# Scores' left factor z of batches 3 to 15 by seven block products instead of eight, a two-slot ring for silu's output, the attention output told by halves, and new orders on every engine

## The reference, cut to what matters

```python
# x: (16, 1024, 256) fp32; all dims 256 except HIDDEN = 768
x = x + layernorm(attn(layernorm(x)))        # qkv = x W^T + b; softmax(Q K^T / 16) V, one head of 256
x = x + layernorm(ffn(layernorm(x)))         # h = silu(x Wg^T) * (x Wu^T); h Wd^T, weights are int32 / 127
```

## Time and profile before

| | |
|---|---|
| median of 3 runs | 1324.28 us (1322.99 to 1324.62) |
| the profiled execution's own time | 1322.73 us |
| its span (first to last instruction) | 1320.9 us |
| PE busy | 1308.1 us of the span |
| ACT, POOL, DVE busy | 1019.5, 997.6, 953.1 us |
| instructions | 23123, of them 7204 matmuls |

### The profile page before, as it was taken

How to read it: one execution, slowest core, us unless ns; L and a number is a source line. 1 busy time by engine, 2 the same in 40 slices (tenths; PEclk the granted TensorE clock), 3 DMA queues, 4 the chain that set the end, 5 groups by cost and what they waited for, 6 DMA issues and landing times.

```text
span 1320.9 us, 23123 instructions
## 1 busy us (share of the span) xinstructions
PE 1308.1 (99%) x7204; PEld 705.6 (53%) x7204; DVE 953.1 (72%) x2670; ACT 1019.5 (77%) x1610; POOL 997.6 (76%) x1081
## 2 busy tenths in 40 slices
PE   8999999999999999999999999999999999999998
PEld 5455455555555555455554555545555555555655
DVE  7877686776867768687686867767687686766566
ACT  6768787788878788787887877878777887867655
POOL 4887687786868868687786877878778686875645
PEclk9999999999999999999999999999999999999999
DMA  6887657676656865578666776666767666666422
GB/s 203 158 172 143 147 93 145 130 153 116 120 124 134 167 119 112 122 138 161 125 115 124 130 148 128 142 124 111 144 128 158 116 119 121 136 132 130 92 64 65
DMA packets 492110, 171.96 MB, mean 130 GB/s; under 512 B 473041, under 2 KB 475473, under 8 KB 491986
## 3 DMA queue, kind: packets, MB, share of 16 engines
q1 hardware_dynamic: 491184, 169.67, 65.1%
q10 hardware_dynamic: 802, 0.79, 0.2%
HBM read 36.70 MB, written 16.78 MB: 40 GB/s over the span
## 4 chain that ended last, share of the span: by engine, by line
PE 90%; POOL 3%; issue 2%; ACT 2%; DMA 2%; SPq 1%; DVE 1%; POOLq 0%; ACTq 0%; DVEq 0%
PE S L1073 71%; PE S L1232 17%; POOL Pl L449 1%; DMA yTl<-yl 1%; SPq L309 1%; DMA PTh<-Ph 1%; POOL qTl L426 0%; POOL yl L476 0%; PE S L1102 0%; PE S L1155 0%; ACT xh L558 0%; SPq L278 0%; ACT P L614 0%; SPq L321 0%; POOL xl L401 0%
## 5 line engine op out<-in xcount | busy, mean ns | idle before, releaser
L449 POOL TENSOR_TENSOR Pl<-P,Ph 128x1024 f16<-128x1024 f32 x128 | 271.4, 2131 | 52.4 <-issue 37.8
L1073 PE MATMUL S<-PTh,xh 128*128 128x512 f16 x512 | 194.1, 379 | 0.0
L1073 PE MATMUL S<-PTl,xh 128*128 128x512 f16 x512 | 194.0, 379 | 0.0
L1073 PE MATMUL S<-PTh,xl 128*128 128x512 f16 x512 | 194.0, 379 | 0.0
L651 ACT ACTIVATE hf<-S,sc 128x512 f32<-128x512 f32 x192 | 129.3, 684 | 64.8 <-PE S L1073 52.8
L614 ACT ACTIVATE P<-P,nmx,sc 128x1024 f32<-128x1024 f32 x112 | 138.2, 1234 | 43.4 <-DVE nmx L901 43.2
L1073 PE MATMUL S<-Wh,hTh 128*128 128x256 f16 x768 | 170.2, 273 | 0.4 <-DVE X L986 0.4
L1073 PE MATMUL S<-Wh,hTl 128*128 128x256 f16 x768 | 170.2, 273 | 0.0
L364 POOL TENSOR_TENSOR rs<-rs,mhalf 128x4 f32<-128x4 f32 (+2 forms) x160 | 146.0, 912 | 13.3
L485 POOL TENSOR_TENSOR hTl<-hf,hTh 128x512 f16<-128x512 f32 x128 | 146.8, 1157 | 8.6 <-ACT hTh L658 5.6
L895 DVE CUSTOM_DVE_ANT_0 P<-S,P 128x512 f32<-128x512 f32 x112 | 76.9, 689 | 96.7 <-ACT P L581 46.6
(11 more groups left out here) (206 smaller groups left out, 3295.6 us busy)
## 6 DMA issues: line engine op xcount, KB each, us to landing
xs<-in_L_attn_t SPq DMA_DIRECT2D x32, 512.0 KB, 4.6
X<-in_L_attn_t SPq DMA_DIRECT2D x32, 512.0 KB, 4.6
out_x<-X SPq DMA_DIRECT2D x62, 256.0 KB, 2.9
PTh<-Ph SPq DMA_TRANSPOSE x128, 3.7
PTl<-Pl SPq DMA_TRANSPOSE x128, 3.3
hTh<-in_L_ffn_w_up SPq DMA_DIRECT2D x1, 768.0 KB, 6.9
hTl<-in_L_ffn_w_down SPq DMA_DIRECT2D x1, 768.0 KB, 8.4
hTl<-in_L_ffn_w_gate SPq DMA_DIRECT2D x1, 768.0 KB, 9.8
```

The source lines that it names most:

```text
L449: p.engine.tensor_tensor(out=Pl[:, m % 3, :], in0=P[:, m % 4, :], in1=Ph[:, m % 3, :], op=ALU.subtract).then_inc(pl_vector if i in PL_ON_V ...
L1073: done = t.engine.matmul(out, s, m, start=(start and i == 0), stop=(stop and i == len(terms) - 1))
```

## The change

1. **z of batches 3 to 15 by seven block products.** `z_part` (eight block products of three passes) gives way to `z_first`, `z_second`, `z_third`, `z_last` (seven). Their inputs are blocks of A, four mixes of A (Bh, Bl, made once) and the mixes of x that the scores already need. The sums of the products are put together by three new copies on ACT (`z_copy`) and four sums on DVE (`z_sum`, in place of four `z_bias`). The four blocks of z lie in banks 0 to 3 together.
2. **Once, in the head:** `A_sum`, `mix_A`, `mixed_low` on POOL and `mixed_high` on ACT make Bh and Bl in hf.
3. **hf has two slots** (the room goes to Bh and Bl), so `silu` of block n waits for block n-2. The down weights are staged in hTh[0] and tTh instead of in hf, and wait for what lay there.
4. **Y_done is told after each half** of `project_v`, and `y_scale` of the first half waits for the first.
5. **Scales** ZS and that of A change by powers of two.
6. **The orders** of SP, POOL, ACT, DVE and of PE from batch 0's FFN on are new (PE's head is the same). The three FFN loads are issued right after batch 0's x; before they stood among the loads of batch 1.

```diff
-        hf = sb("hf", [128, 3, 512])
+        hf = sb("hf", [128, 2, 512])
+        Bh, Bl = sb("Bh", [128, 4, 128], f16), sb("Bl", [128, 4, 128], f16)
...
+        def z_at(g, dj, bank):
+            return ps[:, ((1, 3), (2, 0))[g][dj] if bank is None else bank + dj, :]
+        def zm_wait(e, b, n):
+            e.wait_ge(zm_out, 7 * (b - 3) + (1, 2, 4, 5, 6, 7, 3).index(n) + 1)
+        def block_wait(e, b, g, dj):
+            if b == 2:
+                e.wait_ge(zw_done, 4 * b + 2 * g + dj + 1)
+                return
+            e.wait_ge(z_block, 4 * (b - 3) + ((0, 0), (0, 1), (1, 1), (1, 0)).index((g, dj)) + 1)
...
+        def z_copy(a, b, part):
+            if part < 2:
+                z_words_free(a, b)
+            else:
+                block_wait(a, b, 0, 0)
+            zm_wait(a, b, (1, 6, 7)[part])
+            a.engine.activation(zw[:, part % 2, :], ps[:, 0, :], ACT.Identity, bias=cb[:, part // 2:part // 2 + 1], scale=ZS
+                                ).then_inc(z_copied, 1)
...
-            if n > 2 and (n - 3) % 6 in HL_ON_VECTOR:
-                a.wait_ge(hmul_done, n - 2)
-            elif n > 2:
-                hl_wait(a, (n - 3) // 6, (n - 3) % 6)
+            if n > 1 and (n - 2) % 6 in HL_ON_VECTOR:
+                a.wait_ge(hmul_done, n - 1)
+            elif n > 1:
+                hl_wait(a, (n - 2) // 6, (n - 2) % 6)
...
+        def z_sum(v, b, g, dj):
+            other = zw[:, 1 if (g, dj) == (1, 0) else 0, :]
+            zm_wait(v, b, ((2, 4), (3, 5))[g][dj])
+            v.wait_ge(z_copied, 3 * (b - 3) + ((1, 3), (2, 3))[g][dj])
+            v.engine.scalar_tensor_tensor(out=z_at(g, dj, None), in0=ps[:, 2, :] if g else z_at(g, dj, None), scalar=ZS, in1=other,
+                                          op0=ALU.mult, op1=ALU.add).then_inc(z_block, 1)
...
+        def z_product(t, bank, a, x, ks, di, onto=False):
+            (ah, al), (xh_, xl_) = a, x
+            for sw, mv in pairs((ah, al, xh_[:, ks, di, :], xl_[:, ks, di, :])):
+                done = t.engine.matmul(cols(ps[:, bank, :]), sw, mv, start=not onto, stop=True, skip_group_check=True)
...
+        def z_first(t, b, free0, free1, free2, free3):      # four products: banks 0, 1, 3, 2
...
+        def z_second(t, b):
+            t.wait_ge(z_copied, 3 * (b - 3) + 1)
+            z_product(t, 0, B_block(2), (tTh, tTl), slice(4, 8), 1, True).then_inc(zm_out, 1)
+        def z_third(t, b):
+            t.wait_ge(z_copied, 3 * (b - 3) + 2)
+            z_product(t, 0, B_block(3), (tTh, tTl), slice(4, 8), 0, True).then_inc(zm_out, 1)
+        def z_last(t, b):
+            t.wait_ge(x_turned[1], 32 * b)
+            block_wait(t, b, 1, 1)
+            z_product(t, 2, B_block(4), (xTh[b % 2], xTl[b % 2]), slice(4, 8), 1, True).then_inc(zm_out, 1)
```

More of the change, by code:

```diff
@@ L16 @@
 OS = 2.0 ** -23
-ZS = 2.0 ** -20
+ZS = 2.0 ** -18
 PL_ON_VECTOR = ()
@@ new lines, in _ @@
+            h_high(a, 13, 0, 1)
+            t_high(a, 15, 1)
+            y_hat(a, 13, 1, 0)
+            y_hat(a, 13, 1, 1)
+            silu(a, 13, 0, 2, 0)
+            y_high(a, 13, 1)
+            silu(a, 13, 0, 3, 6)
+            h_high(a, 13, 0, 2, 0)
+            silu(a, 13, 0, 4, 2)
+            h_high(a, 13, 0, 3)
+            h_high(a, 13, 0, 4)
+            silu(a, 13, 0, 5, 6)
+            z_copy(a, 15, 0)
+            h_high(a, 13, 0, 5, 6)
+            z_copy(a, 15, 1)
+            p_high(a, 14, 4)
@@ L2160, in _ @@
             h_rest(v, 0, 0, 5, 0)
-            x_stats(v, 3, 0)
-            h_mul(v, 0, 1, 0, 6)
+            o_low(v, 1, 0, 0)
+            h_mul(v, 0, 1, 0, 2)
             h_mul(v, 0, 1, 1, 0)
-            z_rest(v, 2, 1, 2)
+            x_stats(v, 3, 1)
+            d_stats(v, 0, 0, 1)
+            row_inverse(v, 1, 1)
             d_stats(v, 0, 0, 0)
-            h_mul(v, 0, 1, 2, 0)
-            mix_queries(v, 2, 1, 2)
-            h_mul(v, 0, 1, 3, 6)
-            h_rest(v, 0, 1, 2, 0)
@@ L2209, in _ @@
             x1_add(v, 1, 1, 1)
-            z_bias(v, 3, 0, 6)
-            sum_12(v, 2, 3)
-            h_mul(v, 1, 0, 0, 0)
-            z_rest(v, 3, 0, 6)
-            d_stats(v, 0, 1, 0)
-            h_mul(v, 1, 0, 1, 2)
-            mix_queries(v, 3, 0, 6)
-            d_stats(v, 0, 1, 1)
-            h_mul(v, 1, 0, 2, 0)
-            h_mul(v, 1, 0, 3, 2)
-            d_add(v, 0, 1, 0)
-            h_rest(v, 1, 0, 2, 0)
-            h_mul(v, 1, 0, 4, 6)
-            z_bias(v, 3, 1, 2)
-            h_mul(v, 1, 0, 5, 0)
@@ L2275, in _ @@
                 x1_add(v, b + 1, 1, 1)
-                z_bias(v, b + 3, 0, 6)
-                sum_12(v, b + 2, 3)
-                h_mul(v, b + 1, 0, 0, 0)
-                d_stats(v, b, 1, 0)
-                z_rest(v, b + 3, 0, 6)
-                h_mul(v, b + 1, 0, 1, 2)
-                mix_queries(v, b + 3, 0, 6)
-                h_mul(v, b + 1, 0, 2, 0)
-                h_mul(v, b + 1, 0, 3, 2)
-                h_rest(v, b + 1, 0, 2, 0)
-                d_stats(v, b, 1, 1)
-                row_inverse(v, b + 2, 0)
@@ L2288, in _ @@
-                d_add(v, b, 1, 0)
-                h_mul(v, b + 1, 0, 4, 6)
-                h_mul(v, b + 1, 0, 5, 0)
-                d_add(v, b, 1, 1)
-                h_rest(v, b + 1, 0, 5, 0)
-                h_mul(v, b + 1, 1, 0, 6)
-                h_mul(v, b + 1, 1, 1, 0)
-                z_bias(v, b + 3, 1, 2)
-                z_rest(v, b + 3, 1, 2)
-                d_stats(v, b + 1, 0, 0)
-            h_mul(v, 13, 1, 2, 0)
-            mix_queries(v, 15, 1, 2)
-            h_mul(v, 13, 1, 3, 6)
@@ L2301, in _ @@
-            d_stats(v, 13, 0, 1)
+                h_mul(v, b + 1, 0, 0, 6)
+                h_mul(v, b + 1, 0, 1, 0)
+            sum_12(v, 14, 3)
+            d_stats(v, 12, 1, 0)
+            d_stats(v, 12, 1, 1)
+            h_mul(v, 13, 0, 2, 0)
+            h_mul(v, 13, 0, 3, 6)
+            h_rest(v, 13, 0, 2, 0)
+            h_mul(v, 13, 0, 4, 2)
+            h_mul(v, 13, 0, 5, 6)
+            d_add(v, 12, 1, 1)
+            h_rest(v, 13, 0, 5, 6)
+            z_sum(v, 15, 0, 0)
+            d_add(v, 12, 1, 0)
@@ new lines, in _ @@
+            z_sum(v, 15, 0, 1)
+            z_sum(v, 15, 1, 1)
+            h_mul(v, 13, 1, 0, 6)
+            z_rest(v, 15, 0)
+            z_sum(v, 15, 1, 0)
+            mix_queries(v, 15, 0)
+            h_mul(v, 13, 1, 1, 6)
+            d_stats(v, 13, 0, 0)
+            z_rest(v, 15, 1)
+            mix_queries(v, 15, 1)
+            d_stats(v, 13, 0, 1)
+            h_mul(v, 13, 1, 2, 6)
+            row_inverse(v, 14, 0)
+            h_rest(v, 13, 1, 2, 6)
+            row_inverse(v, 14, 1)
```

1214 lines of the change are left out of this document (635 added, 579 removed).

## The result

The changed kernel takes 1332.2 us (median of 6 runs, 1331.5 to 1334.3), the kernel before it 1323.0 beside it (6 runs, 1321.9 to 1324.6): ratio 1.0076, 95% interval 1.0065 to 1.0086. It is slower by 0.76%: 9.2 us by the two medians, 10 by the ratio. I had forecast 5.9 us less and a range up to 1325. The profiled execution has a span of 1329.8 us against 1320.9.

A forecast was written before the change was run, and what follows sets the result against it. PE's instruction count was taken to bound the kernel. -8.4 - 0.45 - 0.9 + 1.8 + 1.6 + 0.5 = -5.9 us on 1322.7 gave 1316.9, plus 1.5 to the median: 1318.4 us, range 1314 to 1325.

The forecast's parts named there:

- 39 matmuls, -8.4: PE's z products: three fewer matmuls of 0.216 us in each of 13 batches, 8.4 us less.
- New close places, +1.8: Barely late signals at the new order's tight waits: 0.15 us a pass, x 12, 1.8 us more (between 0 and 6).
- nine holds of 0.05, -0.45: PE starting 0.05 us behind its slot at 256.07, a hold in nine passes: gone, 0.45 us less.
- the hold on yl's transpose, -0.9: PE's earlier wait on y's low transpose, at gate_up(0, 0): now 3 us margin, credited 0.9 us less.
- batch 13, +1.6: Once, in batch 13: PE waits 0.9 us ahead of z_third and 0.7 ahead of z_last, 1.6 us more.
- head, +0.5: PE's branch into the FFN part waits for SP's later last FFN transpose: 0.5 us more (0 to 2).
- Y by halves, 0: Y_done by halves moves the first half's scale 1.3 us earlier; bound 0 to 1.3 us, taken as 0.
- table loads: ACT's tail: four more loads for exp, 35 instead of 31, 5.2 us of ACT, hidden, 0 for PE.
- from the profiled execution to the median, +1.5: The median of runs lies 1.5 us above the profiled execution: 1316.9 becomes 1318.4 us.
- Rival 3: z block holds PE each pass, at z_last and gate_up(1, 3): about 0.4 us x 12 = 4.8, 1323.2 us; chance 0.12.
- Rival 4: Silu of blocks 3 and 5 hangs on POOL's order; PE loses 1.0 us at gate_up(1, 0) each pass: 1330.4; chance 0.12.
- the ring: hf's two slots: silu waits for block n-2; margins 1.3 and 1.1 us; if overrun, 12 us in all.

The follow-up runs named there:

- the tile 5 run: Changed kernel with SP issuing softmax tile 5's high-word transpose 24 us earlier, tile 6's low word before tile 7's high word, a store later: 1331.7 us, ratio 1.0069.
- the first of the two last kernels: Changed kernel with the loop's order edits for gate_up, softmax transposes and down, plus new orders in head, batch 13 and batch 14; down(b, 0, 0) uncut: 1332.1 us, ratio 1.0083.
- the fetches moved: Changed kernel with 40 waits on an already met semaphore added at the start of TensorE's program, to shift its instruction fetches: 1332.9 us, ratio 1.0075.

## Why the prediction was wrong, step by step

- *39 matmuls, -8.4*: right. 7165 matmuls, and the loop with its holds mended has a pass of 79.94 us, 0.1 over the 79.8 of matmuls that I gave.
- *New close places, +1.8*: this term failed; it measured about 11 in the loop. The step was the layout that asked of each wait whether its signal comes in time: it took every step at its nearest row, and left whole waits out. Of the places that I listed, attend_part(b+1, 0, 0) was late by 0.17, not 0.1 (2.0 us). gate_up(b, 0, 5) had a margin of 1.3 by my layout; it had none in four passes, since t_high(b+2, 1), which waits for a transpose and stands ahead of h_high on ACT, isn't in that layout: the item names POOL's queue alone. Two places weren't on the list: down(b-1, 1, 0), which is due 4.75 us after project_v(b, 1)'s end where it was 6.3 before, as twelve matmuls of z and pair_second no longer stand between, and one more gate_up does (4.5 us, 4.1 of it in the loop); and the softmax's transposes (3.1 us, 1.8 of it in the loop). For the transposes the prediction had named the gap itself: it had checked SP's order only for y and the FFN weights.
- *nine holds of 0.05, -0.45*: wrong in sign. They stood at down, and became the 0.26 to 0.65.
- *the hold on yl's transpose, -0.9*: gone from its place; by the holes it was three holds, 1.2 us. At batch 14 0.85 and 0.59 us went as well, which I hadn't counted, but 0.97 at project_v and 0.77 in the tail came.
- *batch 13, +1.6*: 0.94 and 0.83 by name, as worked out, and 0.7 more.
- *head, +0.5*: 2.1 us, the top of its own range.
- *Y by halves, 0*: for a kernel with these orders it is worth 27.6 us; I had costed it on one chain.
- *table loads*: 35, as counted, and no hold at the tail's new places for exp.
- *from the profiled execution to the median, +1.5*: that was the chance of three runs. The kernel before has a median of 1323.0 in six, 0.3 above that execution.
- *Rival 3*: neither mixing nor z_last held PE (0.16 us twice in the loop). *Rival 4*: silu of block 3 was indeed the late one, but PE lost time at gate_up(b, 0, 5) and not at gate_up(b, 1, 0), and the ring costs 1 to 1.5 us, not 12. That its 1330.4 lies near the result is luck.

So the mechanism of the gain was right and the price of the new close places was mis-sized: 1.8 us in the sum, some 11 in the loop of the trace, and the rest at the two ends.

## What to carry to other kernels

When the bounding engine has hardly a hole, lay out every wait of the new order, not only those next to the edit, and beside each margin write what else is due in it: a transfer's landing has a spread that an engine's instruction hasn't, here 0.8 to 1.8 us. Work removed from between two steps shortens the slack of the chain that ran beside it: ask of each removed item what was hidden under it. And mend one hold at a time with the trace in hand, reading the event ahead of the waiting instruction too; two of my three guesses at the ends named the wrong signal.

## What the runs showed of the hardware

- A 16 KB instruction fetch that begins 1.0 to 2.3 us behind the issue of a DMA transpose makes it land 0.8 to 1.8 us later (15 of 15 passes; 33 of 33 without one took 3.04 to 3.24 us). The packet itself takes 0.9 to 1.6 us on one of 16 engines. In the kernel before, a fetch that began 2.5 us behind the issue cost nothing (landing after 3.03) and one at 0.7 us cost 0.4. All this is of t's first transpose in a pass: t's second, which is issued 4 to 6 us later beside a load of x, takes 3.5 to 4.7 us in the changed kernel where no such fetch falls in, so fetches are not the only thing that makes a transpose land late.
- TensorE's granted clock fell to its lower level for some 3.5 us after some holds and not after others that were as long. It fell after the head's 2.2 us (the window of the tile 5 run above) and after its 4.5 us in the first of the two last kernels, where matmuls of 512 columns then stood 0.43 us apart (1.2 GHz) and not 0.216 (windows below); it did not after the changed kernel's 2.1 us at the same place, nor after 2.2 us there with the fetches moved, and of two holds of 2.6 us in batch 13 only one was followed by it, and of two of 2.3 again one. A fall costs about 1.5 us on top of the hold. What decides stays open.

```profile
98.00:102.50 4.50, 0.04 (x1) 0.07 (x2) 0.76 (x1) 3.37 (x5) 4.50 (x4) 0.95 0.81 154
102.50:106.00 3.50, 3.50 (x10) 1.29 (x11) 1.83 (x4) 3.47 (x6) 3.50 (x2) 0.57 1.13 113
106.00:110.00 4.00, 4.00 (x21) 1.78 (x19) 3.75 (x12) 2.10 (x4) 2.94 (x3) 1.00 0.99 199
```
